# Writing the gate tiles from SyncE's queue instead of GpSimd's, in a recurrent attention and mixture-of-experts kernel

## The chip, the cores and the metric

One Trainium2 chip, all 8 cores. Each core gets two of the 16 sequences (4096 tokens of width 1024) and runs the same program on them; no core sends anything to another. The time is that of the slowest core, in microseconds (us). Per core there are five instruction queues, each run in order: TensorE (PE), VectorE (DVE), ScalarE (ACT), GpSimd (POOL) and SyncE (SP). DMA transfers are issued here from two of them, POOL and SP; both feed the core's 16 DMA engines. In the views, SPq and POOLq are the issuing of transfers by those queues.

## The reference

```python
xn = _layernorm(x)
s = attention(xn, qw, kw, vw, ow)        # 16 heads of 64, rope, causal softmax
# gate branch: 8 experts, the best two per token
logits = xn @ Wg.T
vals, sel = top_k(logits, 2); w = softmax(vals)
y = einsum('td,eod->teo', xn, We) + be
g = silu(sum over the chosen two of w * y)
x = x + s * g
```

The kernel computes all 8 experts for every token and weights them, with weight zero for those not chosen.

## The kernel before

The program has three stages, with barriers between them.

Stage 1 (to about 562 us) loads x, normalises it, keeps the transposed normalised tokens in SBUF (`xnT`), projects to q, k and v, applies rope, and writes q, k and v to DRAM buffers (`q_sp` from SP, `k_sp` and `v_sp` from POOL). It ends with the gate logits and the expert weights per token.

Stage 2 is the gate branch, the one that the change touches. Its 32 token tiles of 128 go in four rounds `q4` of eight tiles `t8`. A round has these steps, and every engine's queue holds them in this order:

- Bias: 16 rounds of one small matmul into `PC6` (line 632) and one ACT copy of it into the f32 accumulator `acc32[t8]` (line 637). Each matmul waits for the ACT instruction before it, so matmul and copy alternate. The first of these matmuls also waits for everything that ACT had been given before, the last Silu of the round before included. They use neither expert weights nor SP.
- Four expert groups `eg`, two experts each. A group's weights come from the DRAM copy `we16` by 16 transposing DMAs issued on SP (lines 653 to 656, recorded at line 237), into one of two slots: `eg` 0 and 2 use slot 0, `eg` 1 and 3 slot 1. The first of the 16 waits until the matmuls that last used this slot are done (`slot_free`). The matmuls (line 677) wait for all 16 (`wrd`): 8 tiles x 2 halves x 8 chunks x 2 experts = 256 matmuls of 128x512. After each 16 of them DVE adds the result, weighted, to `acc32` (line 687).
- Gate: for each of the eight tiles an ACT Silu (line 701) from `acc32[t8]` into `g_st[t8 % 2]`, and a store of this 128x1024 f16 tile (256 KB) to the DRAM buffer `g_sp` (line 705, recorded at line 238). There are two buffers, so the Silu of tile t8 waits until the store of tile t8 - 2 has landed (`sgsA`, `sgsB`).

Since SP runs ahead of the compute, the transposes for `eg` 0 of the next round are in its queue right behind those for `eg` 3 of this round, and are let go when the matmuls of `eg` 2 end.

Stage 3 is attention and the output. After the barrier SP loads `ow` (line 713), waiting for the stores of `g_sp`, then k by transposes (line 722); POOL loads v (`v_sp`), the gate (`g_sp`) and x. For each group of 512 queries SP issues 8 transposes of q (`q_sp`) and at its end a 2 MB store of the output, with the next transposes behind it.

Of the kernel before, what the change touches and what calls it, by code (L numbers as in the profile page):

```python
# [107 lines left out]
def build_nc():  # L108
# [20 lines left out]
    g_sp = nc.dram_tensor("g_sp", [T, D], F16, kind="Internal").ap()  # L129
# [3 lines left out]
    with ctx:  # L133
# [5 lines left out]
        def c16(ar, off, cols):  # L139
            return ar[:, off:off + 2 * cols].bitcast(F16)  # L140
# [27 lines left out]
        g_st = [c16(AR2, 98304, 1024), c16(AR2, 100352, 1024)]  # L168
# [65 lines left out]
        def dma(q, out, in_, sem, transpose=False, waits=()):  # L234
            def fn(e, out=out, in_=in_, tr=transpose):
                if tr:
                    return e.dma_start(out, in_, transpose=True)  # L237
                return e.dma_start(out, in_)  # L238
            return W(q, fn, waits=waits, inc=sem, amt=16)
# [388 lines left out]
        for q4 in range(4):  # L628
            for t8 in range(8):
                gt = q4 * 8 + t8  # L630
# [12 lines left out]
            for eg in range(4):  # L643
# [15 lines left out]
                for t8 in range(8):  # L659
                    gt = q4 * 8 + t8  # L660
                    for half in range(2):
# [22 lines left out]
                        for ib, ee in ((0, e0), (1, e1)):  # L684
                            W("vector",
                              lambda e, ib=ib, t8=t8, half=half, PG=PG,
                              gt=gt, ee=ee: e.scalar_tensor_tensor(  # L687
                                  acc32[t8][:, half * 512:(half + 1) * 512],
                                  PG[:, 512 * ib:512 * ib + 512],
                                  wm32[:, gt * 8 + ee:gt * 8 + ee + 1],  # L690
                                  acc32[t8][:, half * 512:(half + 1) * 512],
                                  op0=ALU.mult, op1=ALU.add),
# [4 lines left out]
            for t8 in range(8):  # L697
                gt = q4 * 8 + t8
                p = gt % 2
                sg_ = "sgsA" if p == 0 else "sgsB"  # L700
                W("scalar", lambda e, t8=t8, p=p: e.activation(  # L701
                    g_st[p][:, :], acc32[t8][:, :], AF.Silu),
                  waits=[("eV", C["eV"]), (sg_, 16 * (gt // 2))], inc="eA")
                tok[("accfree", t8)] = C["eA"]
                dma("gpsimd", g_sp[gt * 128:(gt + 1) * 128, :], g_st[p][:, :],
                    sg_, waits=[("eA", C["eA"])])

        P.barrier()
# [292 lines left out]
```

How the kernel before makes its waits and increments, by code:

```python
            def body(eng):  # L84
                for (e, ws, fn, incs) in ops:
                    if e != name:
                        continue
                    for (sn, v) in ws:
                        eng.wait_ge(sems[sn], v)
                    if fn is None:
                        if incs:
                            ins = eng.drain()
                            for (sn, a) in incs:
                                ins.then_inc(sems[sn], a)
                        continue
                    ins = fn(eng)
                    for (sn, a) in incs:
                        ins.then_inc(sems[sn], a)
```

## Time and profile before

| what | us |
|---|---|
| runs | 3116.21 and 2922.74, median 3019.48 |
| the profiled execution, its own time | 2932.47 |
| its span on the slowest core (core 6) | 2930.9 |
| spans of the eight cores | 2872.0 to 2930.9 |
| PE busy | 2209.2 (75%) |
| ACT busy | 963.2 (33%) |
| DVE busy | 995.0 (34%) |
| POOL busy | 478.3 (16%) |
| share of the chain that ended last: PE / ACT / POOL | 61% / 13% / 5% |
| the same: DMA `g_sp` | 2% |

The span runs from the first to the last instruction of a core; the time of a run has a little around it. PE is the busiest engine, and the chain of work that ended last is mostly PE's; 2% of the chain is time in which only a store of `g_sp` was awaited. The table's shares are averages over three different stages; the change concerns the ends of the four rounds of stage 2.

### The profile page before, as it was taken

What the parts mean: (1) busy time and instruction counts of PE and PEld (TensorE: products, weight loads), DVE (VectorE), ACT (ScalarE), POOL (GpSimd) and SP (SyncE); (2) the same over time, 40 slices, a digit from 0 to 9 for tenths busy, and PEclk for the clock granted to TensorE, in tenths of its full rate; (3) what the DMA queues carried; (4) which work ended last, traced back from release to release, by engine and by line L of the source; (5) the groups of instructions that cost most, each with busy time, mean ns of one, the idle gap of its engine ahead of it and who ended that gap; (6) DMA issues with size and microseconds to landing.
All of it is one profiled execution on the core that took longest, in us unless ns stands there. A gap on an engine that the chain in (4) does not pass through costs nothing.

```text
span 2930.9 us, 30318 instructions; the slowest of 8 cores (2872.0 to 2930.9 us)
## 1 busy us (share of the span) xinstructions
PE 2209.2 (75%) x9976; PEld 825.5 (28%) x9976; DVE 995.0 (34%) x1529; ACT 963.2 (33%) x1373; POOL 478.3 (16%) x575
## 2 busy tenths in 40 slices
PE   2887888749986995899499905777788537777787
PEld 0333333514432442344144401111121101121211
DVE  2676666434431442244134401321121213221212
ACT  2443333120001001100200014457668224657584
POOL 0465455400000000000000002111111112211110
PEclk9998779759997998899699955778798756787888
DMA  4298742443352356056415062202010352030100
GB/s 127 82 158 155 144 102 73 101 74 58 58 89 55 58 84 112 6 82 91 86 27 89 1 186 45 72 0 72 1 58 1 95 108 69 4 72 1 58 1 29
DMA packets 380486, 203.95 MB, mean 70 GB/s; under 512 B 342944, under 2 KB 351136, under 8 KB 379824
## 3 DMA queue, kind: packets, MB, share of 16 engines
q1 hardware_dynamic: 365552, 134.37, 23.5%
q0 software_dynamic: 14784, 67.66, 10.6%
q8 instruction: 85, 1.39, 0.2%
q14 instruction: 65, 0.53, 0.1%
HBM read 84.28 MB, written 67.37 MB: 52 GB/s over the span
## 4 chain that ended last, share of the span: by engine, by line
PE 61%; ACT 13%; issue 7%; POOL 5%; SPq 5%; DVE 4%; DMA 4%; POOLq 0%; ACTq 0%; DVEq 0%
PE PA L677 15%; PE PB L677 15%; ACT AR L861 8%; PE PV L780 6%; POOL AR L872 5%; PE PA L906 4%; SPq L237 4%; PE PA L419 4%; PE PC L419 4%; PE PB L419 4%; PE PA L851 2%; DMA g_sp<-AR 2%; PE PB L851 2%; ACT AR L790 2%; ACT AR L637 1%
## 5 line engine op out<-in xcount | busy, mean ns | idle before, releaser
L677 PE MATMUL PA<-AR 128*128 128x512 f16 x2048 | 470.4, 383 | 3.3 <-ACT AR L637 3.3
L780 PE MATMUL PV<-AR 128*128 128x512 f16 (+6 forms) x1280 | 419.0, 418 | 66.8 <-POOL AR L872 66.6
L677 PE MATMUL PB<-AR 128*128 128x512 f16 x2048 | 462.9, 379 | 0.0
L861 ACT ACTIVATE AR<-PA 128x1024 f16<-128x1024 f32 x320 | 303.1, 947 | 253.6 <-PE PA L851 251.2
L851 PE MATMUL PA<-AR 64*128 64x512 f16 x640 | 149.4, 458 | 305.1 <-DMA AR<-q_sp 151.4
L687 DVE SCALAR_TENSOR_TENSOR AR<-PA,wm,AR 128x512 f32<-128x512 f32 x256 | 192.2, 751 | 440.5 <-PE PA L677 226.2
L861 ACT ACTIVATE AR<-PB 128x1024 f16<-128x1024 f32 (+1 forms) x320 | 276.4, 864 | 91.6 <-PE PB L851 90.6
L872 POOL TENSOR_TENSOR AR<-AR,tri 128x256 f16<-128x256 f16 x256 | 170.7, 667 | 824.9 <-ACT AR L861 801.2
L687 DVE SCALAR_TENSOR_TENSOR AR<-PB,wm,AR 128x512 f32<-128x512 f32 x256 | 192.2, 751 | 250.2 <-PE PB L677 232.1
L701 ACT ACTIVATE AR<-AR 128x1024 f16<-128x1024 f32 x32 | 33.2, 1053 | 736.9 <-DVE AR L687 675.6
L677 PEld LDWEIGHTS PA<-AR 128*128 128x128 f16 x2048 | 202.1, 99 | 251.5 <-issue 15.1
L822 DVE TENSOR_TENSOR AR<-AR,PC 64x512 f16<-64x512 f32 x64 | 43.5, 679 | 664.5 <-PE PC L816 663.3
L677 PEld LDWEIGHTS PB<-AR 128*128 128x128 f16 x2048 | 200.4, 98 | 241.6
L419 PE MATMUL PC<-AR 128*128 128x512 f16 x512 | 208.2, 407 | 0.0
L238 POOL DMA_DIRECT2D g_sp<-AR x32 | 17.3, 539 | 1128.4 <-ACT AR L701 1126.3
L419 PE MATMUL PA<-AR 128*128 128x512 f16 x512 | 175.4, 426 | 0.0
L851 PEld LDWEIGHTS PA<-AR 64*128 64x128 f16 x640 | 36.2, 95 | 477.9 <-issue 477.2
L419 PE MATMUL PB<-AR 128*128 128x512 f16 x512 | 163.3, 401 | 0.0
L802 DVE COPY AR<-PV 64x1024 f32<-64x1024 f32 x64 | 77.9, 1217 | 247.0 <-PE PV L780 241.3
L780 PEld LDWEIGHTS PV<-AR 128*128 128x128 f16 (+1 forms) x1280 | 83.2, 104 | 266.1 <-issue 265.8
L906 PE MATMUL PA<-AR 128*128 128x512 f16 x512 | 134.4, 421 | 17.4 <-DVE AR L828 14.9
L851 PE MATMUL PB<-AR 64*128 64x512 f16 x640 | 147.5, 454 | 0.0
(100 smaller groups left out, 1702.5 us busy)
## 6 DMA issues: line engine op xcount, KB each, us to landing
we<-we POOLq DMA_DIRECT2D x8, 2048.0 KB, 23.1
out_c<-AR SPq DMA_DIRECT2D x8, 2048.0 KB, 10.3
v_sp<-AR POOLq DMA_DIRECT2D x32, 264.0 KB, 2.6
AR<-v_sp POOLq DMA_DIRECT2D x2, 4224.0 KB, 26.4
AR<-x_c SPq DMA_DIRECT2D x32, 256.0 KB, 10.1
k_sp<-AR POOLq DMA_DIRECT2D x32, 256.0 KB, 3.9
q_sp<-AR SPq DMA_DIRECT2D x32, 256.0 KB, 2.7
g_sp<-AR POOLq DMA_DIRECT2D x32, 256.0 KB, 5.5
```

The lines of the kernel that those rows point to most:

```text
L237: return e.dma_start(out, in_, transpose=True)
L419: e.matmul(o_, lhs, rhs, start=(c == 0), stop=(c == NCH - 1)),
L677: sl=slots[ib], half=half: e.matmul(PG[:, 512 * ib:512 * ib + 512], lhs, sl[:, c * D + half * 512: c * D + (half + 1) * 512], start=(c == ...
L687: gt=gt, ee=ee: e.scalar_tensor_tensor(acc32[t8][:, half * 512:(half + 1) * 512], PG[:, 512 * ib:512 * ib + 512], wm32[:, gt * 8 + ee:gt * ...
L780: nkc=nkc, p2=p2, mw=mw: e.matmul(PV2[0:mw, 512 * p2 + w0:512 * p2 + 512], v_sb[:, kc * VF + h * VW:kc * VF + h * VW + mw], expb3[sbk][:, ...
L790: W("scalar", lambda e: e.activation(recL[64:65, 0:1024], PV2[64:65, 0:1024], AF.Ln), waits=[("eT", pvmm), ("eA", C["eA"]), ("eA", tok.get ...
L802: W("vector", lambda e: e.tensor_copy(at2[0:64, :], PV2[0:64, 0:1024]), waits=[("eT", pvmm), ("eV", tok.get("atrd", 0))], inc="eV")
L822: W("vector", lambda e, hp=hp: e.tensor_mul(attnT[0:64, hp * 512:(hp + 1) * 512], at2[0:64, 0:512], PC6[0:64, :]), waits=[("eV", tok[("atv ...
L851: pbuf=pbuf, PS=PS, p2=p2: e.matmul(PS[:, 512 * p2:512 * p2 + 512], kT[base:base + 64, ch * S + kc * 128:ch * S + (kc + 1) * 128], qT[pbuf ...
L861: W("scalar", lambda e, PS=PS, sbk=sbk, ev=ev: e.activation(ev(expb3[sbk]), ev(PS), AF.Exp, scale=1.0 / 32.0), waits=[("eT", C["eT"]), ("e ...
L872: W("gpsimd", lambda e, sbk=sbk, tv=tv: e.tensor_mul(tv(expb3[sbk]), tv(expb3[sbk]), tri[:, :].unsqueeze(1).broadcast_to([128, 2, 128])), ...
L906: e.matmul(PA[:, 512 * half:512 * half + 512], attnT[0:128, cp * 512 + jt * 128: cp * 512 + (jt + 1) * 128], ow128[:, cp * D + half * 512: ...
```

## The change

One word: the stores of the gate tiles are issued on SP's queue, where they were issued on POOL's. Their data, their order among themselves, their waits and their semaphores stay. In SP's queue they stand behind the transposes of `eg` 3 of their round and ahead of the transposes of `eg` 0 of the next round (after the last round, ahead of the load of `ow`).

```diff
                 tok[("accfree", t8)] = C["eA"]
-                dma("gpsimd", g_sp[gt * 128:(gt + 1) * 128, :], g_st[p][:, :],
+                dma("sync", g_sp[gt * 128:(gt + 1) * 128, :], g_st[p][:, :],
                     sg_, waits=[("eA", C["eA"])])
```

## Rows read from the trace of the kernel before

**Rows 1.** Busy time by stretch: us, busy (count) by engine, PEclk, DMA share, GB/s
```profile
643.00:866.00 223.00, 222.30 (x1024) 100.22 (x1021) 95.12 (x127) 0.00 (x0) 0.00 (x0) 0.99 0.34 57
866.00:894.00 28.00, 0.28 (x1) 0.10 (x1) 0.98 (x2) 9.51 (x9) 3.78 (x7) 0.53 0.99 189
894.00:917.00 23.00, 9.42 (x18) 1.75 (x18) 0.00 (x0) 9.36 (x16) 0.54 (x1) 0.50 0.24 45
...
1692.00:1712.00 20.00, 0.00 (x0) 0.00 (x0) 1.07 (x2) 8.32 (x8) 4.32 (x8) 0.54 0.27 105
```

**Rows 2.** Waits in stage 2: who waited for whom, us in total, times, longest
```profile
ACT AR L701 <- DMA g_sp<-AR: 61.0, 19, 6.5
```

**Rows 3.** Timeline, end of round 0: start, us, engine, line, [idle before <-releaser]
```profile
868.45 2.00 ACT L701 ACTIVATE AR<-AR 128x1024 f16<-128x1024 f32 x2
...
875.62 2.26 ACT L701 ACTIVATE AR<-AR 128x1024 f16<-128x1024 f32 x2 [5.17 <-DMA g_sp<-AR]
...
892.51 1.06 ACT L701 ACTIVATE AR<-AR 128x1024 f16<-128x1024 f32 x1 [0.40 <-DMA g_sp<-AR]
...
893.72 0.58 PE L632 MATMUL PC<-be16s,wmT 8*128 8x512 f16 x1 [28.42 <-ACT AR L701]
...
916.57 6.45 PE L677 MATMUL PA<-AR 128*128 128x512 f16 x16 [0.82 <-ACT AR L637]
```

**Rows 4.** Timeline of ACT, first and last Silu of rounds 1 and 2
```profile
1142.51 2.00 ACT L701 ACTIVATE AR<-AR 128x1024 f16<-128x1024 f32 x2 [226.09 <-DVE AR L687]
...
1168.15 1.06 ACT L701 ACTIVATE AR<-AR 128x1024 f16<-128x1024 f32 x1 [3.36 <-DMA g_sp<-AR]
...
1417.01 2.00 ACT L701 ACTIVATE AR<-AR 128x1024 f16<-128x1024 f32 x2 [224.69 <-DVE AR L687]
...
1444.56 1.06 ACT L701 ACTIVATE AR<-AR 128x1024 f16<-128x1024 f32 x1 [3.98 <-DMA g_sp<-AR]
```

**Rows 5.** Timeline, end of round 3, with no transposes behind it
```profile
1693.32 2.00 ACT L701 ACTIVATE AR<-AR 128x1024 f16<-128x1024 f32 x2 [224.85 <-DVE AR L687]
1694.91 0.54 POOL L238 DMA_DIRECT2D g_sp<-AR  x1 [248.23 <-ACT AR L701]
...
1697.29 2.10 ACT L701 ACTIVATE AR<-AR 128x1024 f16<-128x1024 f32 x2 [1.96 <-DMA g_sp<-AR]
...
1705.20 2.23 ACT L701 ACTIVATE AR<-AR 128x1024 f16<-128x1024 f32 x2 [1.79 <-DMA g_sp<-AR]
...
1712.08 0.41 SPq L238 DMA_DIRECT2D AR<-ow  x1
```

**Rows 6.** Expert weights: three groups of 16 on SP's timeline; landing, all groups and one
```profile
754.87 24.03 SPq L237 DMA_TRANSPOSE AR<-we  x16
...
1249.40 28.43 SPq L237 DMA_TRANSPOSE AR<-we  x16
...
1415.18 31.98 SPq L237 DMA_TRANSPOSE AR<-we  x16
...
AR<-we SPq DMA_TRANSPOSE x256, 5.1
...
DMA to landing us min/median/max: 4.2/6.1/9.6
```

**Rows 7.** Stage 1: a q tile's last rope step, its store on SP, all 32 landings
```profile
538.92 1.38 DVE L478 TENSOR_TENSOR AR<-AR 128x512 f16<-128x512 f16 x1
...
540.37 10.97 SPq L238 DMA_DIRECT2D q_sp<-AR  x2
...
DMA to landing us min/median/max: 2.0/2.7/22.7
```

**Rows 8.** Stage 3, SP's timeline: transposes issued right behind other large transfers
```profile
1712.54 27.12 SPq L237 DMA_TRANSPOSE AR<-k_sp  x1
...
1864.68 20.29 SPq L237 DMA_TRANSPOSE AR<-q_sp  x8
```

## Prediction

> **What bounds the kernel now.** I read the busy times by stretch first. In a round's four expert groups PE is busy 222.30 of 223 us at a granted clock of 0.99 (its upper level, 2.4 GHz), with the DMA engines at 0.34 [rows 1]. Nothing the change touches can shorten that part. Then come two stretches in which PE does almost nothing: 28 us with 0.28 us of PE and 9.51 us of ACT while the DMA engines are at 0.99, and 23 us with 9.42 us of PE and 9.36 us of ACT at clock 0.50 (its lower level, 1.2 GHz) with the DMA engines at 0.24 [rows 1]. The waits say who is late in the first: ACT's Silus waited 61.0 us in 19 waits for stores of g_sp [rows 2]. The timeline gives the order: Silus in pairs (the two buffers), a wait of about 5 us for a landing after each pair, then the first bias matmul, which had waited 28.42 us for ACT, then 16 bias rounds, then the next expert matmuls [rows 3]. So at the end of a round the path is: DVE's last add, eight Silus paced by store landings, 16 bias rounds, PE. At the same time SP is loading weights, and none of that is waited for: PE's first expert matmul of the round is released by the last bias copy [rows 3].
>
> The Silu stretch, from the first Silu's start to the last one's end, is 868.45 to 893.57 = 25.1 us [rows 3], 1142.51 to 1169.21 = 26.7 and 1417.01 to 1445.62 = 28.6 [rows 4], and in the last round 1693.32 to 1707.43 = 14.1 [rows 5]. The code is the same four times. What differs is that in the first three the 16 transposes for eg 1 of the next round run beside the stores (slot 1 comes free when eg 3 ends), and in the last none do: DMA share 0.99 against 0.27 [rows 1]. This is the row that tells what a store is worth on free DMA engines.
>
> **The change, part by part.** All work that is moved: 32 stores leave POOL and enter SP's queue, eight at each round's end. POOL had nothing else there, so nothing on POOL gains except the end of the stage. On SP the stores wait for the Silus, and behind the waiting stores stand the 16 transposes of the next round's eg 0, then the 16 of its eg 1. Today eg 0's are let go when eg 2 ends, a quarter of the 223 us stretch or some 55 us before the round ends [rows 1], and are landed long before they are needed. After the change they can start only when the last Silu is done and the eighth store is issued.
>
> (a) The Silus. With both sets of transposes held back, the stores have the DMA engines to themselves, as in the last round. A pair's period there is 1697.29 - 1693.32 = 3.97 us [rows 5]: 1.06 Silu, 0.53 to POOL's issue at 1694.91, 2.38 to the next Silu. On SP the lag is shorter: the rope step ends at 538.92 + 1.38 = 540.30 and SP issues at 540.37, 0.07 later; 32 stores of the same size landed in 2.0 us at best and 2.7 at the median, from their issue [rows 7]. I take 2.4, POOL's value, which lies between: period 1.06 + 0.07 + 2.4 = 3.53. Four pairs, the last of 2.2: 3 x 3.53 + 2.2 = 12.8 us; 11.6 with 2.0, and as the other end 14.1, no gain over POOL's undisturbed stores. Saved: 25.1 - 12.8 = 12.3, 26.7 - 12.8 = 13.9, 28.6 - 12.8 = 15.8, and 14.1 - 12.8 = 1.3. Sum 43.3 (38.1 to 48.1).
>
> The Trainium skill (Advanced Engine Details and Errata, section DGE: Hardware vs Software) gives about 600 ns to the first byte for a transfer issued from Sync and about 1 us for one from GpSimd. By that a landing would be 0.4 us shorter than POOL's, which twelve periods (three a round) would turn into some 5 us more saved; that is an estimate from the page, and the trace's best (2.0 against 2.38) agrees with it while its median does not.
>
> (b) The transposes of eg 0. A group's 16 issues take 24.03 to 28.43 us where no store is beside them [rows 6]; the eleven such groups of rounds 0 to 3, of which these are the shortest and the longest, average 26.2, which I take. Beside stores a group took 31.98 [rows 6], the upper end. The landing after an issue has a median of 5.1 us over all groups [rows 6]; since the last issue itself (26.2 / 16 = 1.6) is already counted, 3.4 to 3.5 remain. Lower end 4.2 - 1.5 = 2.7, upper end 6.1 - 2.0 = 4.1. Ahead of the first stand the eighth store's lag and issue, 0.5 us. Behind a store in flight the first transpose may be held: eight q transposes right behind a 2 MB store took 20.29 us [rows 8], 2.5 each against 1.6 for an undisturbed weight transpose. Here only the last one or two 256 KB stores are ahead, so the hold lies between 0 and one landing, 2.4; I take 1.1. Ready after the last Silu's end: 0.5 + 1.1 + 26.2 + 3.4 = 31.2 us (27.2 to 39.0).
>
> What covers it: the 16 bias rounds, which need neither SP nor the weights, from 893.57 to 916.57 = 23.0 us [rows 3]; the two other boundaries have the same 16 rounds. So PE waits 31.2 - 23.0 = 8.2 us longer three times: 24.6 (12.6 to 48). The cover that the load has today, eg 3's matmuls, is gone; without the bias rounds too it would cost 94. Next late would be eg 1's transposes, behind eg 0's: another 26 us of issues, landed at about 31.2 + 26 = 57 after the last Silu, while PE needs them only a quarter of the 223 us stretch [rows 1], some 55, after 31.2: hidden, with 29 us to spare.
>
> PE's restart costs the same: already its clock is 0.50 before the first expert matmuls [rows 1] and the first 16 take 6.45 us [rows 3]; a few more idle us don't change that.
>
> (c) The end of the stage. The last Silu ends at 1707.43 and ow is issued at 1712.08, 4.65 later [rows 5], behind POOL's drain. After: one SP landing, 0.07 + 2.4, so 2.2 us earlier; with what POOL may start earlier I take 2.5 (0 to 4.5).
>
> Sum: 2932.5 - 43.3 + 24.6 - 2.5 = 2911 us, against the profiled execution's own 2932.47. The best ends give 2932.5 - 48.1 + 12.6 - 4.5 = 2892, the worst 2932.5 - 38.1 + 48 = 2942. The median shown, 3019.48, is the middle between two runs 193 us apart, one of them near the profiled execution; the forecast is for an execution like that and the profiled one, which are themselves 10 us apart, so I widen by about 10 below.
>
> **The rivals.** First, slower: the transposes are held behind the stores far longer than one landing. Place: SP's queue at the first transpose of eg 0. The point that decides: the savings are (43.3 + 2.5) / 3 = 15.3 us per boundary, so the change loses as soon as eg 0 is ready later than 23.0 + 15.3 = 38.3 us after the last Silu. For it: the first k transpose, right behind the ow load, sat 27.12 us in its issue [rows 8]. Against it: in that place ow, v, gate and x, some 8 MB of plain transfers, were under way together, here at most two stores of 256 KB. If it held 27 us here, 26 more than I took, the time would be 2911 + 3 x 26 = 2989. The Trainium skill (DMA: Bandwidth & Descriptors, section Rules for kernel authors) says to issue a DMA early, compute, and wait for it late, and the change does the opposite to eg 0. By that rule alone, with nothing beside the load, each boundary would pay all 31.2 and the time would be 2911 + 3 x 23.0 = 2980; the trace speaks against it with the 23.0 us of bias rounds. Both ways together: 0.09.
>
> Second, the change doesn't do what it says: the stores land as slowly as before, because something other than the transposes slows them. For it: one SP store took 22.7 us to land [rows 7]. Against it: the last round's 14.1 us. The load would still be late: 2932.5 + 24.6 - 2.5 = 2955. 0.06.
>
> Third, the load is hidden after all (16 transposes alone on the engines in under 18 us): 2932.5 - 43.3 - 2.5 = 2887. Against it: of all groups none took under 24.03. 0.10.
>
> **How the numbers follow.** My forecast, PE late by some 8 us three times and the Silus faster by more, has 0.72, with its own range 2892 to 2942; 0.03 is left for what I don't see. Predicted: 2911. From 2880 to 2950 the range takes in the forecast, the third rival and the 10 us between executions, and leaves out the other rivals. About 2% of the time, 59 us, is what a measurement of this kernel can tell from no change. Slower by more than that begins at 2991, the far end of the first rival: 0.07. Faster by more than that ends at 2874, below every case worked out: 0.05. Within: 0.88.
>
> **What would show each step.** (a) Silu stretches of 11.6 to 14.1 us at all four round ends, with a store's landing about 2.4 us after its issue. (b) SP's 32 transposes in one run after the last Silu, none before it in that boundary; the first expert matmul of rounds 1 to 3 released by a DMA of the expert weights and not by the last bias copy, 27 to 39 us after the last Silu. (c) ow issued about 2.5 us after the last Silu. Wrong would be: a first transpose of many us on SP, Silu stretches still above 20 us, or the first expert matmuls still released by the bias copy.

## The result, and the profile after

| | kernel before | changed kernel |
|---|---|---|
| median of all runs, us | 2940.22 (40 runs) | 2901.39 (42 runs) |
| profiled execution, us | 2932.47 | 2902.24 |
| slowest core's span in it, us | 2930.9 (core 6) | 2900.7 (core 3) |
| changed / before, undisturbed runs | | 0.9948 (0.9922 to 0.9973) |

In some executions the cores of one die run at a lower granted clock and take some per cent longer; the ratios here leave those out. The ratio says 0.5% less, some 15 us (8 to 23); the two profiled executions lie 30 us apart. Later measurements of the same two kernels gave 0.9881 and 0.9909 (below). The forecast was 2911 us, 21.5 below the profiled execution of before, and no change by the 2% bound.

The round's end, stretch by stretch, on the slowest core (us from the start, length; busy time and count of PE, weight loads, DVE, ACT, POOL; granted clock, DMA share, GB/s):

```profile
865.50:878.00 12.50, 0.22 (x1) 0.10 (x1) 0.00 (x0) 8.45 (x9) 0.00 (x0) 0.50 0.37 141
878.00:900.00 22.00, 9.06 (x16) 1.48 (x15) 0.00 (x0) 8.88 (x16) 0.00 (x0) 0.50 1.02 149
900.00:911.00 11.00, 0.00 (x0) 0.00 (x0) 0.00 (x0) 0.51 (x1) 0.00 (x0) 0.50 1.13 137
911.00:1136.00 225.00, 223.74 (x1024) 100.84 (x1024) 95.38 (x128) 0.00 (x0) 0.00 (x0) 0.99 0.37 56
```

Before, there were two stretches between the expert matmuls: 28 us of Silus with the DMA engines at 0.99, and 23 us of bias with them at 0.24 [rows 1]. Now there are three. The Silus take half as long, with the DMA engines at 0.37. The bias rounds take what they took, but beside full DMA engines (1.02). Then there are 11 us with nothing on PE and the DMA engines still full: the weights. The matmul stretch itself is as before, clock 0.99.

The waits in the same stage, then one line of SP's own (who waited for whom: us in total, times, longest):

```profile
ACT AR L701 <- DMA g_sp<-AR: 14.9, 13, 1.3
...
PE PA L677 <- DMA AR<-we: 23.6, 3, 11.4
```

```profile
SPq L89 <- ACT AR L701: 384.9, 32, 88.6
```

The Silus' wait for stores was 61.0 us [rows 2] and is 14.9. A wait that was not there has come: PE for the expert weights, three times, 23.6 us in all. The line of SP says why: SP stood 384.9 us at the stores, waiting for Silus, with the next transposes behind. At the end of rounds 0 to 2 eg 0's transposes stood behind the last of these waits, with their slot long free.

The timeline of the end of round 0 (start, us, engine, line, what; in brackets the idle time before and what ended it):

```profile
865.87 2.00 ACT L701 ACTIVATE AR<-AR 128x1024 f16<-128x1024 f32 x2
867.00 11.02 SPq L238 DMA_DIRECT2D g_sp<-AR  x8
869.12 2.02 ACT L701 ACTIVATE AR<-AR 128x1024 f16<-128x1024 f32 x2 [1.25 <-DMA g_sp<-AR]
...
875.58 2.06 ACT L701 ACTIVATE AR<-AR 128x1024 f16<-128x1024 f32 x2 [1.21 <-DMA g_sp<-AR]
878.12 37.10 SPq L237 DMA_TRANSPOSE AR<-we  x21
911.21 4.00 PE L677 MATMUL PA<-AR 128*128 128x512 f16 x9 [11.38 <-DMA AR<-we]
...
1177.49 6.16 PE L677 MATMUL PA<-AR 128*128 128x512 f16 x16 [6.22 <-DMA AR<-we]
...
1443.21 6.41 PE L677 MATMUL PA<-AR 128*128 128x512 f16 x16 [6.02 <-DMA AR<-we]
```

A pair's period is 869.12 - 865.87 = 3.25 us and the wait in it 1.25, where it was 5.17 [rows 3]. The last Silu ends at 877.64, and 0.48 us later the first transpose is issued; none stands before it. PE's first expert matmul was released by the last bias copy [rows 3] and is now released by the weights, in all three rounds.

The same over all eight cores, worked out from the timelines, as means of 24 round ends (rounds 0 to 2, 8 cores) in the first and third row and of 8 in the others:

| us | before | after |
|---|---|---|
| first Silu's start to last one's end, rounds 0 to 2 | 24.25 (21.7 to 28.6) | 11.8 |
| the same, round 3 | 14.1 | 11.9 |
| last Silu's end to the first expert matmul | 23.1 | 29.6 (25.2 to 33.9) |
| last expert matmul to the first of attention | 83.0 | 77.0 |

The sum by these: 3 x (24.25 - 11.8) - 3 x (29.6 - 23.1) + (83.0 - 77.0) = 37.4 - 19.5 + 6.0 = 24 us. (The last row holds the last round's Silus.)

### The profile page after: what moved, and what is told of

Read it like the earlier page. It is cut to its first block, busy times and chain, and to the rows that moved or that the text cites. A ratio compares the mean times of both kernels' runs of the same rounds, so it can differ in the third digit from the quotient of the medians.

```text
span 2900.7 us, 30318 instructions; the slowest of 8 cores (2836.4 to 2900.7 us)
## 1 busy us (share of the span) xinstructions
PE 2208.3 (76%) x9976; PEld 825.8 (28%) x9976; DVE 994.5 (34%) x1529; ACT 962.9 (33%) x1373; POOL 461.3 (16%) x543
## 4 chain that ended last, share of the span: by engine, by line
PE 61%; ACT 12%; SPq 7%; issue 7%; POOL 5%; DVE 4%; DMA 3%; ACTq 0%; POOLq 0%; DVEq 0%
PE PA L677 16%; PE PB L677 15%; ACT AR L861 8%; SPq L237 7%; PE PV L780 6%; POOL AR L872 5%; PE PA L906 4%; PE PA L419 4%; PE PC L419 4%; PE PB L419 4%; PE PA L851 2%; PE PB L851 2%; ACT AR L790 2%; PE PV L359 1%; DMA AR<-c_sin 1%
## 5 line engine op out<-in xcount | busy, mean ns | idle before, releaser
L677 PE MATMUL PA<-AR 128*128 128x512 f16 x2048 | 472.6, 385 | 24.4 <-DMA AR<-we 23.6
```

Of the source, the lines that this page charges most:

```text
L677: sl=slots[ib], half=half: e.matmul(PG[:, 512 * ib:512 * ib + 512], lhs, sl[:, c * D + half * 512: c * D + (half + 1) * 512], start=(c == ...
```

## The experiments

**Which part makes the stores fast, and which makes PE late.** The change does three things at once: it takes POOL's way of issuing out of the path, it takes the transposes from beside the stores, and it puts eg 0's transposes late. Four kernels, all on one chip, set these apart. The first keeps the stores on POOL and holds eg 0's transposes, and so eg 1's behind them, until the last Silu:

```diff
--- the kernel before
                        ("scsC", C["scsC"]), ("scsD", C["scsD"])]
+                if q4 > 0 and eg in (0,):
+                    ldw.append(("eA", tok[("accfree", 7)]))
```

> Stores stay on POOL as before; the transposes of the next round's eg 0 (and so of eg 1 behind them) wait for the last Silu of the round. Theory (the stores were slow because transposes ran beside them): all four Silu stretches about 14.1 us, PE's first expert matmul some 7 to 8 us late three times; sum -38 + 23, some 15 us below before, ratio about 0.995. Rival (SP's issue path is what made the stores fast): Silu stretches stay at 25 to 29 us in rounds 0 to 2, the loads are late all the same, some 23 us above before, ratio about 1.008.

Measured 0.9947 (0.9928 to 0.9965), 15 us below before. On its timeline, at the end of round 1:

```profile
1093.12 2.00 ACT L703 ACTIVATE AR<-AR 128x1024 f16<-128x1024 f32 x2 [230.70 <-DVE AR L689]
...
1105.08 2.02 ACT L703 ACTIVATE AR<-AR 128x1024 f16<-128x1024 f32 x2 [1.96 <-DMA g_sp<-AR]
...
1107.17 49.18 SPq L237 DMA_TRANSPOSE AR<-we  x32
...
1134.61 5.63 PE L679 MATMUL PA<-AR 128*128 128x512 f16 x16 [5.03 <-DMA AR<-we]
```

From 1093.12 to 1107.10 the Silus take 14.0 us, with the stores on POOL: taking the transposes away gives 24.25 - 14.0 = 10 of the change's 12.4 us, and SP's shorter way only the other 2.2. PE starts on the weights 28.3 us after the last Silu (mean of 24).

The second also keeps POOL, and holds only eg 1's transposes (the same two lines with `(1,)`), so that eg 0's come early as before.

> Stores stay on POOL; only the transposes of the next round's eg 1 wait for the last Silu, eg 0 comes early as before. Theory (transposes beside the stores cost the Silus their time, and eg 1 has room): Silu stretches about 14.1 us, no load late, eg 1 landed some 31 us after the last Silu and needed after 78; some 38 us below before, ratio about 0.987. Rival (SP's issue path): Silu stretches unchanged, ratio 1.000.

Measured 0.99 (0.9877 to 0.9922), 29 us below before. Silus 13.9 to 14.3 us on every core, and PE released by the bias copy again:

```profile
1097.95 2.00 ACT L703 ACTIVATE AR<-AR 128x1024 f16<-128x1024 f32 x2 [224.79 <-DVE AR L689]
...
1111.13 1.06 ACT L703 ACTIVATE AR<-AR 128x1024 f16<-128x1024 f32 x1 [0.24 <-DMA g_sp<-AR]
1112.26 23.62 SPq L237 DMA_TRANSPOSE AR<-we  x16
...
1135.48 5.48 PE L679 MATMUL PA<-AR 128*128 128x512 f16 x16 [0.82 <-ACT AR L637]
```

Its transposes are issued in a group of 16 right after the Silus; nothing waits for them. So it is eg 1's transposes that slowed the stores, and eg 1 has the room to come later. 3 x (24.25 - 14.05) = 31 us by the stretches agrees with 29.

The third issues the stores from ACT's queue and leaves all transposes where they were:

```diff
--- the kernel before
-                dma("gpsimd", g_sp[gt * 128:(gt + 1) * 128, :], g_st[p][:, :],
+                dma("scalar", g_sp[gt * 128:(gt + 1) * 128, :], g_st[p][:, :],
```

> Stores issued on ACT's own queue, transposes where they were before: eg 0 early, eg 1 beside the stores. Theory (contention with the transposes): Silu stretches stay at 22 to 29 us in rounds 0 to 2, no load late, ratio 0.995 to 1.005. Rival (a store not issued by POOL lands fast whatever runs beside it): Silu stretches about 13 us in all rounds, some 45 us below before, ratio about 0.985.

Measured 0.996 (0.9946 to 0.9975). Its Silu stretches are 19.2 to 25.4 us in rounds 0 to 2 and 12.3 to 13.1 in the last:

```profile
1093.26 28.19 SPq L237 DMA_TRANSPOSE AR<-we  x16
1095.12 1.06 ACT L701 ACTIVATE AR<-AR 128x1024 f16<-128x1024 f32 x1 [225.91 <-DVE AR L687]
1096.25 0.34 ACTq L238 DMA_DIRECT2D g_sp<-AR  x1
...
1101.98 1.06 ACT L701 ACTIVATE AR<-AR 128x1024 f16<-128x1024 f32 x1 [4.23 <-DMA g_sp<-AR]
```

A store issued on ACT's queue is slow all the same with 16 transposes beside it: the Silu waited 4.23 us, against 1.25 in the changed kernel. The rival, that a store not issued by POOL lands fast whatever runs beside it, falls. The mean of the stretches is 21.4 us, below the 22 to 29 that were expected: leaving POOL's queue is worth 2 to 3 us of a stretch (24.25 - 21.4 here, 14.0 - 11.8 between the first of these kernels and the changed one). Stores from SP's own queue with transposes beside them were not run.

The fourth keeps the stores on SP and puts eg 0's transposes of the next round into SP's queue ahead of them (the 16 issues made a function, called for eg 0 ahead of the Silu loop):

```diff
--- the changed kernel
+        def load_we(eg):
...
             for eg in range(4):
...
+                if not (q4 > 0 and eg == 0):
+                    load_we(eg)
...
                 slot_free[sp] = C["eT"]
+            if q4 < 3:
+                load_we(0)
             for t8 in range(8):
```

> Stores on SP as in the change, but the transposes of the next round's eg 0 are put into SP's queue ahead of them. Theory (the change's loss is SP's order alone): Silu stretches about 12 us, the first expert matmul released by the last bias copy again, some 22 us below the changed kernel and 48 below before, ratio about 0.984. Rival (PE is late for another reason, or early transposes slow the Silus again): no faster than the changed kernel, ratio about 0.995.

Measured 0.9851 (0.9828 to 0.9873), 43 us below before. Silus 11.6 to 12.1 us everywhere, and PE is not late:

```profile
1086.52 2.00 ACT L710 ACTIVATE AR<-AR 128x1024 f16<-128x1024 f32 x2 [225.91 <-DVE AR L694]
...
1096.18 2.03 ACT L710 ACTIVATE AR<-AR 128x1024 f16<-128x1024 f32 x2 [1.20 <-DMA g_sp<-AR]
1098.70 81.47 SPq L237 DMA_TRANSPOSE AR<-we  x17
...
1121.51 5.61 PE L684 MATMUL PA<-AR 128*128 128x512 f16 x16 [0.82 <-ACT AR L652]
```

The row of 17 are eg 1's 16 and, much later, the first of eg 2. By the stretches 37.4 + 6.0 = 43.4 us, by the measured ratio 43. The two kernels differ in the order of SP's queue and in nothing else, so this order costs the change what PE is late in its traces: 14 to 20 us by the stretches (3 x 4.8 to 3 x 6.5).

**What covers the late weights.** The prediction took 23.0 us of bias rounds as the cover. Here the rounds alternate between two PSUM banks (PC6 and PC7, buffers that the bias matmul writes), so that matmul and copy overlap, and the first two matmuls of a round need no longer wait for the last Silu; once in the changed kernel and once in the version with eg 0 ahead:

```diff
--- the changed kernel
+                    PBI = PC6 if half == 0 else PC7
...
-                      waits=[("sbe", bew), ("eA", C["eA"])], inc="eT")
+                      waits=[("sbe", bew),
+                             ("eA", tok.get(("bifree", half), C["eA"]))],
+                      inc="eT")
```

> The changed kernel with the 16 bias rounds alternating between two PSUM banks (PC6 and PC7), so that matmul and copy overlap and the rounds take some 12 us in place of 23. Theory (in rounds 1 to 3 the bias rounds only cover the weights, which are ready 29.6 us after the last Silu): PE's wait for the weights grows from 6.5 to about 17, its start after the last Silu stays at 28 to 31, only round 0 gains, some 11 us below the changed kernel, ratio about 0.988. Rival (the bias rounds are on the path and the weights only wait beside them): all four rounds gain, 44 us below the changed kernel, ratio about 0.977.

> Stores on SP, eg 0's transposes queued ahead of them, and the same two banks for the bias. Theory: no weights are waited for, so all four rounds gain some 11 us over the version with eg 0 ahead alone (0.985), ratio about 0.970; eg 1's transposes, landed some 30 us after the last Silu, still come before PE needs them (some 67). Rival (the weights are late again once the cover shrinks): at most 11 us gained, ratio about 0.981.

On the changed kernel: 0.9862 (0.984 to 0.9885), where the changed kernel on the same chip had 0.9881. On the version with eg 0 ahead: 0.9717 (0.9665 to 0.9769). One and the same edit brings 6 us there (11 were expected, and the intervals of the two overlap) and some 39 here (0.9851 to 0.9717, from two chips; 44 were expected). The waits of the changed kernel with it, and its first expert matmul of round 2:

```profile
PE PA L681 <- DMA AR<-we: 56.2, 3, 20.3
```

```profile
1125.63 5.90 PE L681 MATMUL PA<-AR 128*128 128x512 f16 x16 [18.53 <-DMA AR<-we]
```

The bias rounds got 12 us shorter (23.0 to 11) and PE's wait for the weights 12 us longer (5.6 to 17.4 on the mean of 24); the first expert matmul starts 26.1 to 31.0 us after the last Silu as before. So beside late weights the bias rounds are cover, and without them they are path.

**What is left of a Silu pair.** Stores on SP, eg 0 ahead, four gate buffers `g_st` in place of two (and four semaphores):

```diff
--- the version with eg 0 ahead
-        g_st = [c16(AR2, 98304, 1024), c16(AR2, 100352, 1024)]
+        g_st = [c16(AR2, 98304 + 2048 * i, 1024) for i in range(4)]
...
-                p = gt % 2
-                sg_ = "sgsA" if p == 0 else "sgsB"
+                p = gt % 4
+                sg_ = "sgs" + "ABCD"[p]
```

> Stores on SP, eg 0's transposes ahead, and four gate buffers in place of two. Theory (what is left of a Silu pair's period is the store's landing): a Silu waits for a store four tiles back, landed long before, so the stretch is 8 x 1.06 = 8.5 us in place of 11.8; four times 3.3, some 13 us below the version with eg 0 ahead alone, ratio about 0.981. Rival (the stores queue up behind each other, so that the landing grows with more in flight): stretch stays at 11 to 12, ratio 0.985.

Measured 0.979 (0.9766 to 0.9814), where 0.981 was expected. The Silu stretch is 7.7 us in all 32 round ends; no Silu waits for a store any more.

**All of it together**: eg 0 ahead, two banks for the bias, four gate buffers.

> Stores on SP, eg 0's transposes queued ahead, two banks for the bias, four gate buffers. Theory (the round's end is a chain, and each part is shortened by itself): Silu stretch 7.7 us and PE's start 11.3 after it, 4 x 4.1 = 16 us below the version without the four buffers (0.9717), ratio about 0.966. Rival (with so little left, eg 1's transposes or the stores' landings become late): ratio 0.971 or above, with a wait for weights or stores in the trace.

Measured 0.9638 (0.9619 to 0.9657), 105 us below before and clearly below both of the kernels that it is put together from. That is a little more than the 0.966 expected, which was worked out from 0.9717, a ratio known to 0.005. Its whole round end, from a first Silu to the next expert matmul, is 1078.68 - 1059.71 = 19.0 us where that of before was 916.57 - 868.45 = 48.1 [rows 3]:

```profile
1059.71 7.68 ACT L714 ACTIVATE AR<-AR 128x1024 f16<-128x1024 f32 x8 [225.90 <-DVE AR L698]
1060.84 6.94 SPq L238 DMA_DIRECT2D g_sp<-AR  x8
1067.87 27.47 SPq L237 DMA_TRANSPOSE AR<-we  x16
1078.68 5.09 PE L688 MATMUL PA<-AR 128*128 128x512 f16 x16 [0.87 <-ACT AR L655]
```

**How much the change brings.** The first ratio, 0.9948, gives 15 us where the stretches give 24. So the changed kernel was measured twice more, and the kernel before once against itself.

> The changed kernel as it is, once more, on one chip beside the next three. By the stretches of its first trace (mean of eight cores against before: Silus 3 x 12.4 shorter, expert matmuls 3 x 6.5 later, the start of attention 6 earlier) it should be about 24 us below before, ratio about 0.992; by the first measurement's ratio, 0.9948, 15 us.

> The changed kernel a third time, beside the kernel before of the next run. Its first two ratios, 0.9948 and 0.9881, lie outside each other's intervals, while the stretches of both traces give the same 24 us (0.992). If the difference is one between chips or jobs, this one falls somewhere from 0.988 to 0.995, with Silu stretches of 11.8 us and the weights ready 28 to 30 us after the last Silu again.

> The kernel before against itself, for a second trace of it. Ratio 1.000. If the stores' slowness beside the transposes is a matter of sharing the DMA engines, the Silu stretches of rounds 0 to 2 are again 22 to 29 us and differ from core to core, and those of round 3 are 14 on all cores; if the first trace's slowest core was a rare case, 24 on all.

Measured 0.9881 (0.9861 to 0.9901) and 0.9909 (0.988 to 0.9937), and 1.0003 (0.9974 to 1.0031) for before against itself. In both new traces of the changed kernel PE starts 27.9 us after the last Silu on the mean, against 29.6 in the first trace, which makes 5 us; by the stretches 3 x 12.5 - 3 x 4.8 + 6 = 29 us, 0.990. In the second trace of before the Silu stretches were 22.4 to 26.1 us in rounds 0 to 2 and 14 in round 3: core 6 of the first, with 25.1, 26.7 and 28.6 [rows 3, 4], has the longest of sixteen (26.8 on the mean). The stretches of the first trace give 24 us, so what the first ratio lacks has to be looked for outside the changed part. The span and clock of three cores in the first trace of the changed kernel, and the first and last starts of the expert matmuls on two of them:

```profile
core 2: 2895.0 us, clock 0.842
core 3: 2900.7 us, clock 0.844
...
core 6: 2866.5 us, clock 0.855
```

```profile
L677 PE MATMUL PA<-AR x2048: 379/379/634, 639.8 to 1663.4; 128*128 128x512 f16 x187
```

```profile
L677 PE MATMUL PA<-AR x2048: 379/379/634, 604.9 to 1632.8; 128*128 128x512 f16 x187
```

Core 3 (the first of the two rows) comes 35 us later than core 6 to its first expert matmul and needs no longer from there to the last (1023.6 against 1027.9 us). The slowest core is slowest by what happened to it in stage 1. The rows of 200 to 400 us there, for core 3 and core 6 (length; busy time and count of PE, weight loads, DVE, ACT, POOL; granted clock, DMA share, GB/s):

```profile
200.00:400.00 200.00, 169.22 (x717) 71.84 (x716) 130.76 (x222) 81.87 (x182) 114.58 (x111) 0.87 0.83 157
```

```profile
200.00:400.00 200.00, 171.15 (x795) 75.18 (x793) 136.20 (x243) 89.86 (x199) 124.91 (x119) 0.98 0.89 167
```

PE is busy as long on both, but core 3 has a mean granted clock of 0.87 and gets 717 matmuls done, core 6 0.98 and 795. Cores 6 and 7 in the first trace of before are the same case: 0.83 in this stretch, and their first expert matmul comes at 642.5 and 643.1 us, against 600.0 to 616.1 on the other six. Core 2 beside core 3 (0.87) is the fourth; every other core of all thirteen traces has 0.96 to 1.00 there. So a late pair goes with a lower clock in stage 1, which the change doesn't touch; what lowers it there is open. In 17 of the 23 executions of the changed kernel that the first ratio rests on, the slowest core is more than 20 us above the median of its eight cores; in the two later measurements this holds for one of eight. Such late cores can move a ratio by about 1%, as much as the change itself. That they make the difference between 0.9948 and 0.9881 is argued from these numbers, not shown: for the kernel before in the first measurement the single cores are not on record.

## Why the prediction was right, step by step

**The Silus** (predicted 12.8 us a stretch, 11.6 to 14.1): 11.8 on nearly all. The landing on SP is 2.1 us at the median on the slowest core, nearer the best of the q stores (2.0) than POOL's 2.4 that I took. The lag from the Silu's end to SP's issue is 0.07, as read from the rope step [rows 7]. So a stretch is 1 us shorter than predicted. The sum of what is saved is smaller all the same, for another reason: 43.3 us was worked out on core 6, the slowest, whose Silus were the slowest of all. On the mean of the cores it is 37.4 + 2.2 = 39.6.

**Why the stores were slow**: read from the last round, where no transposes ran [rows 5]. The kernels with POOL's stores and held transposes show it: 14.0 us in every round.

**The late weights** (predicted 31.2 us after the last Silu, 27.2 to 39.0; 24.6 us lost in all): 29.6 on the mean of the first trace and 23.6 us of waits on its slowest core; 27.9 in the other two, some 14 us of loss. Two terms were too large. The 1.1 us taken for a hold behind the last store: the first transpose after the stores took 1.22 to 1.26 us to issue, no longer than an undisturbed one. And the 26.2 us for 16 issues: 25.4 on the mean of the first trace, 23.9 in the other two. The first rival (a hold of many us behind the stores) is out, and so are the second (stores as slow as before) and the third (no wait for the load). PE's restart cost what it did: 6.16 to 6.41 us for the first 16 matmuls of rounds 2 and 3, 6.45 before [rows 3].

**The cover**: the 16 bias rounds, as taken. The two-bank runs show that they are cover in the changed kernel and nowhere else.

**The rule on issuing early.** The Trainium skill (DMA: Bandwidth & Descriptors, section Rules for kernel authors) says to issue a DMA early, compute and wait late. The runs agree for eg 0: putting its transposes back ahead of the stores gave 0.9851 against 0.988 to 0.995. They don't for eg 1, whose transposes were early for nothing and cost the stores their time. The rival that was worked out by this rule alone, 2980 us with nothing beside the load, is out as well: of the 29.6 us the bias rounds covered some 23.

**The end of the stage** (predicted 2.5 us): ow is issued 1683.76 - 1681.13 = 2.63 us after the last Silu, where it was 4.65 [rows 5]; attention starts 6.0 - 2.2 = 3.8 us earlier beyond the Silus' part, within the 0 to 4.5. The earlier issue of ow makes 2.2 of it (4.69 to 2.52 us on the mean of the cores); where the rest comes from was not followed.

**The sum**: -21.5 us forecast, 8 to 23 measured first, then 34 and 26, with 24 and 29 by the stretches. All within 2%, and faster. The mechanism came out as forecast. That the number came so near is in part luck: the Silus' savings were put 3.7 us too high and the late weights 5 us too high (10 by the later traces), and these errors go against each other. The level of 2911 us is luck too: it starts from an execution whose slowest core was already some 40 us late when stage 2 began, and the first measurement of the changed kernel had such cores as well. In the two later measurements both kernels took less, 2853 to 2875 us for the changed one and 2883 to 2916 for before, so the difference holds there and the level doesn't.

## What to carry to other kernels

A queue that runs in order ties together what has nothing to do with each other: ask of each transfer that is moved what stands behind it while it waits, and how long that can afford to stand. Here a move gained because it pushed a bulk load out of the way of small stores that ACT waited for, and lost half of it because it pushed out the wrong load as well. Before a price is taken from the slowest core, look at the same stretch on the others: that core may be the slowest by the very thing that is priced.

## What the runs showed that was not expected

Eight Silus in a row took 7.7 us with four buffers, 0.96 each, where one by itself takes 1.06: I had put 8.5. PE's first expert matmul came 25.2 to 33.9 us after the last Silu over cores and rounds of one execution, the low end below the 27.2 that I had taken as the best. The DMA engines were full on all of them while these weights were loaded (share 0.96 and more), but moved 144 to 193 GB/s; why a core gets less at full engines is not shown.
